# A lead group of columns through the two cross-attention fronts, and the second context split from a turned copy instead of by TensorE transposes

## The reference

```
def _mha(x, y, ...):                      # first cross attention: y = context
    xn, yn = _ln(x, ...), _ln(y, ...)
    q, k, v = xn @ wq, yn @ wk, yn @ wv   # 16 heads
    a = softmax(q @ k.T * D ** (-0.5))
    x_out = x + (a @ v) @ li1_w + li1_b
    h = gelu(_ln(x_out) @ li2_w + li2_b)
    return x_out + h @ li3_w + li3_b
...
qh, kh, vh = (q @ Wq + bq), (k @ Wk + bk), (v @ Wv + bv)   # second: k = v = context, as it is
attn = softmax(qh @ kh.T / sqrt(8)); out = attn @ vh; return concat(out) @ Wo + bo
```

## Time and profile before

| | |
|---|---|
| runs | 698.76, 697.91, 696.05 us; median 697.91 |
| the profiled execution | 696.02 us, of which the profile's span is 694.2 us |
| TensorE clock granted | 0.999 of full speed |
| PE busy | 642.1 us, 92% |
| DVE / ACT / POOL busy | 500.0 / 336.9 / 340.4 us |
| first front (queries to first scores) | about 112 to 136.6 us |
| chunks of `cross1` | 136.6 to about 338 us |
| second front | about 424 to 450.8 us |
| chunks of `cross2` | 450.8 to about 657 us |

### The profile page before, as it was taken

One profiled execution on the slowest core, in us unless ns is written; L12 is line 12 of the kernel. 1 busy time (PEld: TensorE's weight loads), 2 busy tenths in 40 slices (PEclk: granted clock), 3 DMA queues, 4 the chain that ended last, 5 costly groups with the idle time before them and its releaser, 6 DMA issues.

```text
span 694.2 us, 20149 instructions
## 1 busy us (share of the span) xinstructions
PE 642.1 (92%) x8946; PEld 483.4 (70%) x8946; DVE 500.0 (72%) x815; ACT 336.9 (49%) x503; POOL 340.4 (49%) x256
## 2 busy tenths in 40 slices
PE   8788987999999999999998888899999999998997
PEld 4576785677777777777776567567777777776774
DVE  3666733888888888887465761878988988888443
ACT  2153465066456456454354337076466465464443
POOL 1351363087696696664220313066776766845400
PEclk9999999999999999999999999999999999999999
DMA  9600003000000000000030000000000000000000
GB/s 263 225 1 2 3 2 128 1 2 2 3 2 2 2 2 2 3 2 2 2 130 22 0 1 1 1 2 2 2 2 2 2 2 2 3 2 1 3 1 13
DMA packets 3506, 14.74 MB, mean 21 GB/s; under 512 B 372, under 2 KB 628, under 8 KB 3420
## 3 DMA queue, kind: packets, MB, share of 16 engines
q1 hardware_dynamic: 3420, 13.46, 5.8%
HBM read 13.23 MB, written 0.23 MB: 19 GB/s over the span
## 4 chain that ended last, share of the span: by engine, by line
PE 66%; DVE 13%; ACT 9%; POOL 6%; issue 4%; DMA 1%; POOLq 0%; DVEq 0%; ACTq 0%
PE psum L911 16%; PE psum L820 8%; PE psum L869 5%; PE psum L198 5%; PE psum L862 5%; DVE scratch L997 4%; PE psum L864 4%; POOL scratch L982 3%; PE psum L802 1%; PE psum L826 1%; PE psum L811 1%; PE psum L667 1%; POOL nrm L1079 1%; ACT scratch L942 1%; PE psum L672 1%
## 5 line engine op out<-in xcount | busy, mean ns | idle before, releaser
L982 POOL TENSOR_TENSOR scratch<-scratch 125x896 bf16<-125x896 f32 x136 | 232.4, 1720 | 133.0 <-ACT scratch L970 132.5
L970 ACT ACTIVATE scratch<-psum 125x896 f32<-125x896 f32 x192 | 174.0, 918 | 192.5 <-PE psum L911 190.7
L997 DVE TENSOR_REDUCE scratch<-psum 128x1 f32<-128x500 f32 x336 | 210.6, 672 | 16.9 <-PE psum L820 8.5
L911 PE MATMUL psum<-scratch 128*125 128x448 bf16 (+1 forms) x768 | 177.2, 355 | 4.0 <-issue 3.7
L820 PE MATMUL psum<-scratch 128*128 128x500 bf16 x336 | 126.2, 376 | 4.9 <-ACT scratch L945 3.0
L911 PEld LDWEIGHTS psum<-scratch 128*125 128x125 bf16 (+1 forms) x768 | 97.3, 136 | 34.6 <-issue 4.3
L862 PE MATMUL psum<-tok,scratch 125*128 125x65 bf16 x1344 | 109.0, 195 | 1.8 <-DVE kT L1042 1.8
L864 PE MATMUL psum<-tok,scratch 125*128 125x64 bf16 x1344 | 108.4, 192 | 0.0
L862 PEld LDWEIGHTS psum<-tok,scratch 125*128 125x128 bf16 x1344 | 95.6, 97 | 14.0 <-issue 2.6
L864 PEld LDWEIGHTS psum<-tok,scratch 125*128 125x128 bf16 x1344 | 90.4, 99 | 14.4
L198 PE MATMUL psum<-w_second 128*128 128x256 bf16 x712 | 94.3, 272 | 0.0
(11 more groups left out here) (293 smaller groups left out, 803.0 us busy)
## 6 DMA issues: line engine op xcount, KB each, us to landing
raw<-ctx_dram SPq DMA_DIRECT2D x4, 672.0 KB
w_third<-fifth_dram SPq DMA_DIRECT2D x3, 636.0 KB, 5.2
w_third<-third_dram SPq DMA_DIRECT2D x2, 844.0 KB, 21.2
w_third<-third_dram SPq DMA_DIRECT2D x2, 843.5 KB, 19.4
w_fourth<-fourth_dram SPq DMA_DIRECT2D x3, 542.5 KB, 6.1
w_first<-first_dram SPq DMA_DIRECT2D x1, 996.0 KB, 4.9
w_second<-second_dram SPq DMA_DIRECT2D x1, 834.0 KB, 7.0
w_third<-fifth_dram SPq DMA_DIRECT2D x1, 636.5 KB, 8.4
```

Of the source, the lines that this page charges most:

```text
L911: mm = nc.tensor.matmul(bank(S + f, HALF, CP), lhs[0:rows, CP * c:CP * c + CP], rhs[0:rows, HALF * f:HALF * f + HALF], start=(rows == 128) ...
L970: nc.scalar.activation(CR["p"][0:CP, n % RING, :].rearrange("p (f n) -> p f n", f=2), psum[0:CP, S:S + 2, 0:HALF], ACT.Exp).then_inc(self. ...
L982: ops.tensor_tensor(CR["pl"][0:CP, n % RING, :], CR["p"][0:CP, n % RING, :], p_high(n % RING), ALU.subtract).then_inc(done, 1)
L997: nc.vector.tensor_reduce(mxp[:, r, t:t + 1], bank(B, TB), X_AXIS, ALU.max).then_inc(self.aux_freed, 1)
```

## The change

Three things are done at once.

1. **A lead group.** The halves of norms 3, 4, 5, 10 and 11 and of two MLPs become columns 0 to 111 (batches 0 and 1, "lead") and 112 to 447 (the rest). The lead columns go through norm, MLP, queries, Q and the M units first (`lead_pe`, `lead_queries_pe`, `front_pe`, `front_dve_run`); the rest's norm and query matmuls (`rest_queries_pe`, 336 columns each) are put between the M units of batch 0. In the self attention 30 and 16 `keep_warm` matmuls become 4 and 0, and `cross1`'s T units of batch 0 move to just behind the last self-attention output.
2. **The tokens of the context.** `tok` has 4 buffers instead of 3. GpSimd's splits move from chunks 1 and 2 to chunks 11 and 0. Squares, variances and reciprocal roots of context groups 2 and 3 move: group 2 before the first self-attention exponential, group 3 to chunks 3 (ScalarE, square), 5 (VectorE, sum) and 8 of `cross1`'s batch 0.
3. **The turned context.** A copy of the context with channels on the partitions (twice, 128 x 12000 floats) is handed in as `turned_dram` and loaded batch by batch into three buffers over `nrm`. In `cross2` the T units are gone. In chunks 0 and 1 ScalarE makes two copies of 64 x 750 instead of one of 128 x 750 (`context_act`), and VectorE subtracts (`context_dve`) in chunks 1 and 2. For batch 0 this stands in the last batch of `cross1`.

```diff
+        def parts_of(k):
+            return LEAD if k in (3, 4, 5, 10, 11) else HALVES
...
-                keep_warm((6, 30)[p == 3], 7)
+                keep_warm((6, 4)[p == 3], 7)
...
-                keep_warm(WARM_D if p < PAIRS - 1 else 16, 7)
+                keep_warm(WARM_D if p < PAIRS - 1 else 0, 7)
...
+                pe.wait_ge(*ready[0])
+                ups(0, range(4))
+                pe.wait_ge(*ready[1])
+                ups(1, (0, 1))
+                downs(0, range(4))
+                ups(1, (2, 3))
+                centre()
+                downs(1, (0, 1))
+                variance()
+                downs(1, (2, 3))
...
+            def context_act(self, act, b, k):
+                i, cols = b % 2, slice(CTX // 2 * k, CTX // 2 * (k + 1))
...
+                nc.scalar.activation(CR["ya", i][64:128, cols], turned[b % TURNED][64:128, cols], ACT.Copy)
+                nc.scalar.activation(CR["yb", i][0:64, cols], turned[b % TURNED][0:64, cols], ACT.Copy
+                                     ).then_inc(self.ya_set, 1)
+            def context_dve(self, dve, b, k):
...
+                nc.vector.tensor_tensor(CR["ya", i][0:64, cols], turned[b % TURNED][0:64, cols], CR["yb", i][0:64, cols],
+                                        ALU.subtract).then_inc(self.yb_set, 1)
...
+                    if self is cross2 and b < BATCH - 1 and c < 2:
+                        self.context_act(act, b + 1, c)
...
+                    if self is cross2 and b < BATCH - 1 and c in (1, 2):
+                        self.context_dve(dve, b + 1, c - 1)
...
-                    if c in (1, 2) and b < BATCH - 2:
+                    if c == 0 and b < BATCH - 2:
+                        if b == 0:
+                            self.split_tokens(pool, 2, 0)
+                        self.split_tokens(pool, b + 2, 1)
+                    if c == CHUNKS - 1 and b < BATCH - 3:
...
+            cross1.front_pe(pe, q2_act, q2_dve, {
+                ("Q", 1): [lambda: cen_pe(pe, 5, 1, xa, both(ln_b, "xb"))], ("M", 1): [lambda: var_pe(pe, 5, 1)],
+                ("M", 7): [rest(0)], ("M", 9): [rest(1)], ("M", 11): [rest(2)], ("M", 14): [rest(3)]})
```

503 lines of the change are left out of this document (341 added, 162 removed).

## The result

The changed kernel takes 716.92 us (median of 4 runs, 716.21 to 719.11) against 697.63 us for the kernel before (4 runs, 696.05 to 698.76). The ratio is 1.0283, with an interval of 1.0253 to 1.0314: it is slower by 19.3 us. The forecast was 699.5 us in a range of 690 to 710. The profiled run took 716.73 us, its span is 714.9 us (694.2 before).

What follows compares the result with a forecast made beforehand. TensorE, busy 92% of the span, was taken as the bound, with ScalarE's chain ahead of `cross2`'s M 0. Terms +18.6 + 1.0 - 4.3 - 8.4 + 2.5 - 1.7 - 6.0 = +1.7 gave 699.5 us, range 690 to 710.

Steps and rivals of the forecast that it cites:

- self attention and first front, to M 0: From the end of self attention to the first front's M 0: 108.7 instead of 121.44 us, -12.7, of which 4.3 self attention.
- given back in the first front: Behind the first front's M 0: M units, rest queries and a mean product take 14.5 us against 12.4, +2.5 us.
- `cross1`, first scores to first scores of its last batch: `cross1`'s batches: splits leave a waited-for place, -3.3 us; sum of squares +1.3, copies for `cross2` +0.3; together -1.7 us.
- second front: to M 0, given back: Front before `cross2`: M 0 at 427.3 against 435.17 us, -7.9; +1.9 given back behind it; net -6.0 us (4 to 8).
- M 0's delay: In `cross2`, ScalarE's copies (1.7 us) and VectorE's second subtraction (0.94) delay M 0 by 2.65 us in seven batches: +18.6 us.
- contention at the shift row: In `cross2`, GpSimd's moved splits slow VectorE's second halves of the shift row by 0.3 us a batch: +1.0 us (0 to 2).
- Clock: Rival: TensorE's clock falls to 1.2 GHz behind the idle stretch ahead of `cross2`'s M 0, + 7 x 2 = 714 us; chance 0.08.
- The lead order: Lead columns first in both fronts: -8.4 us in the first before +2.5 given back, -6.0 us net in the second.
- The marks: Signs in `cross2`'s profile: periods 29.3 to 29.8 us, M 0 at 11.1 to 11.6, PE waiting some 3 for second `context_dve`.

Runs made afterwards that it cites:

- `splits_later`: The changed kernel with both of GpSimd's splits in `cross2` moved behind a batch's first scores instead of around the batch border: 713.8 us.
- `warm`: The changed kernel with `keep_warm` products that nobody reads filling TensorE's idle stretches in `cross2`: 709.92 us.
- `three_all`: The changed kernel with one 128 x 750 ScalarE copy per half, the second `context_dve` ahead of the Q remainders, splits behind the first scores: 715.61 us.
- `lead_later`: The changed kernel with `cross2`'s context turned by TensorE again and GpSimd's `cross2` splits back at the places of the kernel before: 684.11 us.

## Why the prediction was wrong

By its own terms, each measured in the traces (positive is slower). The first scores of `cross1` stand at 127.16 instead of 136.62 us.

| term | predicted | measured |
|---|---|---|
| self attention and first front, to M 0 | -12.7 | -12.0 |
| given back in the first front | +2.5 | +2.5 |
| `cross1`, first scores to first scores of its last batch | -1.7 (with the last batch) | -1.5 |
| second front: to M 0, given back | -7.9, +1.9 | -6.6, +1.6 |
| M 0's delay in `cross2` | +18.6 | +21.4 |
| contention at the shift row | +1.0 | +5.1 |
| clock in `cross2` | 0 | +8.5 |
| clock behind `cross2` (not of the change) | 0 | +1.6 |

- **Which step failed.** The sum took nothing for TensorE's clock. The rival "Clock" was given 0.08, on "All 40 slices at full clock speak against, gaps of up to 2.2 us among them". The clock fell in every batch and cost 8.5 us, the largest part of the 18.9 us that separate the forecast's +1.7 from the span's +20.6; without it the kernel would have taken some 708.4 us (an estimate, 716.9 - 8.5), inside the range. The stall that the forecast itself placed ahead of M 0 is enough for the fall (`splits_later`), but in two of the seven batches the clock fell only at the border, beside the contention of the next point. The other parts of the 18.9 are 4.1 us at the border, 2.8 of M 0's delay, 1.9 in what stands ahead of `cross2`'s first scores, and the 1.6 behind it, which are chance. The rows of before had single gaps amid dense work; they could not answer for a stall of 3 to 4 us per batch, in which PE is busy for 0.13 of 2.60 us. The rival's own price (one chunk doubled, 7 x 2 = 14 us) was too high; that part of the slow time falls on an idle PE is the likely reason, not shown apart. The Trainium skill, TensorE: Matmul & The Clock Gate, section What's actually happening, was the warning: activity releases the throttle and its lack brings it back. The trace of `warm` agrees: filled stalls, clock 1.00, 8.5 us less in `cross2`.
- **Contention at the shift row** was mis-sized: forecast at +0.3 us on two instructions per batch by a factor of 1.35 from a low part, measured 1.03 us at five borders, factors of 1.8 and 3.0 on the two instructions (0.76 for 0.42, 1.05 for 0.35). In the rows above the add that starts at 530.43 ends at 531.48, 0.2 us behind GpSimd's split (531.27), and in `three_all` the slowed copy ends 0.2 us behind GpSimd's low part; so it seems that a short instruction is held until the long one beside it is done, and a factor from a long row doesn't carry over to a short one. The cause (GpSimd beside it) is shown by `splits_later` and `lead_later`, this reading of its size is only argued from these rows.
- **M 0's delay** had the right mechanism and nearly the right size: 3.05 us per batch instead of 2.65. ScalarE's part is 2.17 instead of 1.7, since four copies of 0.83 us stand end to end (3.3 us, the forecast's own upper bound was 3.2); VectorE's is 0.85 for 0.94.
- **The lead order** was right within 2 us: the second front gained 5.0 net for 6.0, the first 9.5 for 10.2 with the self attention. `cross1`'s batches took 26.0 us, not 25.6. The 0.65 us of the late low part were gained (M 0 to next first scores 17.5 for 18.12), but the splits now stretch VectorE's low parts of chunks 0 and 1 (1.38 for 1.09 and 1.48 for 1.39 us), and M 0 stands 0.33 us later (8.48 for 8.15). No run leaves the lead order, or the fewer `keep_warm` matmuls, out alone: these gains are read from the two traces, and their parts are not measured apart.
- **The marks.** M 0 stood 11.64 to 11.68 us behind the first scores in six batches, just over the 11.1 to 11.6 given, and at 12.42 in one. PE's wait was split in two in five batches: 0.9 or 2.5 us for the first Q remainder and up to 1.0 us ahead of M 0; only in the first batch was it one wait for `context_dve`, of 3.75 us. The period of 29.3 to 29.8 came out at 30.8 to 32.7; the mark "PEclk digits under 9 there (clock)" is the one that fired.

Together the change is a gain of 16 us ahead of `cross2`'s first scores, most of it by the lead order and the shorter `keep_warm`, and in `cross2` a loss of 30 us from the turned context (clock included) and 5 from the splits. The forecast had the first right and the second at 18.6 of 30.
